# An experts' block in two stages: logits of all pairs first, most shared experts beside softmax and top-k

## The reference, cut to what matters

```
x = x + layernorm(mamba(layernorm(x)))          # ends with  y @ out_proj_w
h = layernorm(x)                                # (32, 256, 128)
scores = softmax(h @ gate_w.T)                  # 16 experts
topk_w, topk_idx = top_k(scores over the tokens, 32)
out = scatter_add of (gelu(x_tok @ Wg.T) * (x_tok @ Wu.T)) @ Wd.T * topk_w
shared = (gelu(h @ Ws_g.T) * (h @ Ws_u.T)) @ Ws_d.T
x = x + layernorm(out + shared)
layernorm(v) = (v - mean(v)) / sqrt(var(v) + 1e-5)
```

## Time and profile before

| | us |
|---|---|
| three runs | 1463.27 median (1461.69 to 1469.29) |
| the profiled execution | 1461.25 |
| its span, first to last instruction | 1459.2 |
| mamba and what is before it | 0 to 947.7 |
| the block under change | 947.7 to 1129.1 |
| gather, experts, scatter | 1129.1 to 1459.2 |

### The profile page before, as it was taken

How to read it: one execution, slowest core, us unless ns; L and a number is a source line. 1 busy time by engine, 2 the same in 40 slices (tenths; PEclk the granted TensorE clock), 3 DMA queues, 4 the chain that set the end, 5 groups by cost and what they waited for, 6 DMA issues and landing times. The chain is left out here.

```text
span 1459.2 us, 16108 instructions
## 1 busy us (share of the span) xinstructions
PE 1097.3 (75%) x4121; PEld 509.5 (35%) x4128; DVE 1149.3 (79%) x1531; ACT 887.4 (61%) x1588; POOL 862.9 (59%) x447
## 2 busy tenths in 40 slices
PE   4667777777778867877877865548886889999891
PEld 2312222222222222222222221125554336666791
DVE  6589999999999999999999999776757962222486
ACT  3656666666666666656656654324431876666894
POOL 0389989989989989989989989511101740000003
PEclk9979889889888889889889887769978999999896
DMA  5753853753752753753852755100000001111003
GB/s 153 170 113 69 173 108 69 172 108 68 172 111 65 172 110 66 172 108 68 172 111 66 173 110 122 57 12 1 1 0 1 21 1 35 41 33 42 0 0 115
DMA packets 48434, 122.76 MB, mean 84 GB/s; under 512 B 5776, under 2 KB 20880, under 8 KB 42256
## 3 DMA queue, kind: packets, MB, share of 16 engines
q1 hardware_dynamic: 46816, 121.01, 36.7%
q10 hardware_dynamic: 1584, 1.36, 0.3%
HBM read 83.55 MB, written 5.24 MB: 61 GB/s over the span
## 5 line engine op out<-in xcount | busy, mean ns | idle before, releaser
L551 POOL TENSOR_TENSOR states<-b_dup,dup 128x1024 f32<-128x1024 f32 x256 | 595.6, 2357 | 59.6 <-DMA dup<-dd 59.6
L638 DVE TENSOR_TENSOR_SCAN da<-da,states 128x1024 f32<-128x1024 f32 x176 | 396.2, 2284 | 51.0 <-ACT da L393 44.4
L393 ACT ACTIVATE da<-dup,decay 128x510 f32<-128x510 f32 x512 | 326.0, 671 | 0.0
L291 PE MATMUL yp<-states,fold 128*64 128x512 f32 x1024 | 274.5, 662 | 15.1 <-DVE states L570 8.8
L530 POOL TENSOR_TENSOR states<-states,X 128x1024 f32<-128x1024 f32 x80 | 188.1, 2351 | 92.0 <-DVE states L638 89.7
L570 DVE TENSOR_TENSOR states<-da,X 128x1024 f32<-128x1024 f32 x176 | 211.3, 1201 | 0.0
L389 ACT ACTIVATE da<-zeros 128x4 f32<-128x4 f32 x193 | 33.4, 173 | 289.9 <-DVE states L570 289.5
L638 DVE TENSOR_TENSOR_SCAN states<-da,states 128x1024 f32<-128x1024 f32 x80 | 182.5, 2282 | 14.0 <-ACT da L393 14.0
L1570 POOL TENSOR_TENSOR X<-X,xhT x4 | 12.0, 2995 | 250.3 <-DVE xhT L1550 250.3
L1428 DVE TENSOR_TENSOR hx<-glx,upx 128x512 f32<-128x512 f32 x64 | 41.3, 684 | 126.6 <-ACT glx L1393 118.2
L291 PEld LDWEIGHTS yp<-states,fold 128*64 128x64 f32 x1024 | 68.1, 148 | 206.4 <-issue 184.2
(11 more groups left out here) (184 smaller groups left out, 1798.5 us busy)
## 6 DMA issues: line engine op xcount, KB each, us to landing
b_dup<-bc_rows SPq DMA_DIRECT2D x32, 1024.0 KB, 9.6
dup<-dd SPq DMA_DIRECT2D x128, 256.0 KB, 10.4
X<-bc_rows SPq DMA_DIRECT2D x64, 512.0 KB, 8.8
out<-X SPq DMA_DIRECT2D x4, 1024.0 KB, 5.2
wg<-in_wgT SPq DMA_DIRECT2D x16, 128.0 KB, 2.1
wu<-in_wuT SPq DMA_DIRECT2D x16, 128.0 KB, 2.1
wd<-in_wdT SPq DMA_DIRECT2D x16, 128.0 KB, 2.2
bc_rows<-bcf SPq DMA_DIRECT2D x16, 64.0 KB, 1.6
```

The costliest lines, as they stand in the source:

```text
L291: last = nc.tensor.matmul(yp[64 * i:64 * i + 64, :], fold[:], states[:, (2 * step + i) % RING, s, :], start=False, stop=(q == 3 and s == S ...
L393: ins = nc.scalar.activation(factors[:, s, :].rearrange("p (b t) -> p b t", b=2)[:, :, 1:S], src[:, :, 1:S], ACT.Exp, scale=decay[:, col:c ...
L551: nc.gpsimd.tensor_tensor(states[:, i % RING], b_dup[:, par, s0:s0 + SPI, :], dup[:, par, 1, h, g, :].unsqueeze(1).broadcast_to([P, SPI, N ...
L638: nc.vector.tensor_tensor_scan(to.rearrange("p s t -> p (s t)"), factors.rearrange("p s t -> p (s t)"), ring.rearrange("p s t -> p (s t)") ...
```

## The change

Eight things are changed.

- In the Mamba block the mean over its 128 output columns is taken off each row of w_out, by four VectorE instructions at the program's start (semaphore `centred`). Each token's O then has mean zero, and the layer norm of O is a scaling.
- `statistics_o` makes only a variance; `norm_o` on VectorE is gone. Group 0 is done by 16 `scalar_tensor_tensor` on VectorE (X = O * rstd + X). Groups 1 to 3 are done on POOL, four `tensor_scalar` and one add per pair (`residual`).
- `statistics_o` runs ahead of its group: group 1 before the first pair, groups 2 and 3 after pairs 0 and 2.
- tp has two banks. The transposed pairs stay for all 16 pairs, in xhT at the place of O (`hT(n)`).
- Transposes and logits of all 16 pairs go first. Beside them TensorE does one shared pair in three (pairs 0 to 4; EARLY = 5).
- The other 11 shared pairs run beside softmax, top-k and the expansion of the indices. `down(m-1)` stands between the two halves of `gate_up(m)`.
- The slot matmuls stand before the last shared pair, and their PSUM place is in the bank of the logits.
- Loops are written out.

The diff, cut:

```diff
@@ mamba, VectorE
             nc.vector.tensor_scalar(decay[:], decay[:], 60.0, None, ALU.min).then_inc(decay_ready, 1)
+            nc.vector.tensor_reduce(w_mean[:], w_out[:], AX.X, ALU.add).then_inc(centred, 1)
+            dve.wait_ge(centred, 1)
+            nc.vector.tensor_scalar(w_mean[:], w_mean[:], 1.0 / DM, None, ALU.mult).then_inc(centred, 1)
+            dve.wait_ge(centred, 2)
+            for c in range(2):
+                nc.vector.tensor_scalar(w_out[:, c, :], w_out[:, c, :], w_mean[:, c:c + 1], None, ALU.subtract).then_inc(centred, 1)
@@ experts, POOL
+                def residual(g):
+                    pool.wait_ge(ro_ready, g + 1)
+                    pool.wait_ge(x_back[2 * g // G4], 16)
+                    for n in range(GP * g, GP * g + GP):
+                        for t in range(CH * n, CH * n + CH):
+                            o = O[:, t // 2, t % 2, :]
+                            nc.gpsimd.tensor_scalar(o, o, rstdo[:, t:t + 1], None, ALU.mult).then_inc(on_ready, 1)
+                        pool.wait_ge(on_ready, CH * (n - GP) + CH)
+                        gx = X[:, CH * n:CH * n + CH, :].rearrange("p (b c) d -> p b c d", c=2)
+                        nc.gpsimd.tensor_tensor(gx, gx, O[:, 2 * n:2 * n + 2], ALU.add).then_inc(x_ready, 1)
...
+                for g in range(1, G4):
+                    residual(g)
@@ experts, ScalarE
+                for n in range(PAIRS):
+                    g = n // GP
+                    turned(n)
+                    if n % GP == 1 and g < G4 - 1:
+                        nc.scalar.preload_act_table_set(LOG_EXP)
+                        inverse_x(g + 1)
+                        if g < G4 - 2:
+                            inverse_o(g + 2)
+                    if n % 3 == 2:
+                        for h in range(FH):
+                            gelu(n // 3, h)
+                    if n > 3 and n % 3 == 1:
+                        evacuate(n // 3 - 1)
@@ experts, VectorE
-                def norm_o(g):
-                    dve.wait_ge(ro_ready, g + 1)
-                    for t in range(GT * g, GT * g + GT):
-                        o = O[:, t // 2, t % 2, :]
-                        nc.vector.tensor_scalar(o, o, mvo[:, t, 0:1], rstdo[:, t:t + 1], ALU.subtract, ALU.mult
-                                                ).then_inc(on_ready, 1)
...
+                for t in range(GT):
+                    nc.vector.scalar_tensor_tensor(X[:, t, :], O[:, t // 2, t % 2, :], rstdo[:, t:t + 1], X[:, t, :],
+                                                   ALU.mult, ALU.add).then_inc(x0_ready, 1)
                 statistics_x(0)
+                statistics_o(1)
+                for n in range(PAIRS):
+                    g = n // GP
+                    norm(n)
+                    if n:
+                        take_logits(n - 1)
+                    if n > 3 and n % 3 == 1:
+                        products(n // 3 - 1)
+                    if n % GP == 1 and g < G4 - 1:
+                        statistics_x(g + 1)
+                    if n in (0, 2):
+                        statistics_o(2 + n // 2)
...
+                for r in range(rounds):
+                    products(EARLY + 1 + r)
+                    for g in range(GROUPS):
+                        round_of(r, g)
@@ experts, TensorE
+                turn(0)
+                for n in range(PAIRS):
+                    if n + 1 < PAIRS:
+                        turn(n + 1)
+                    logits(n)
+                    if n % 3 == 2:
+                        for h in range(FH):
+                            gate_up(n // 3, h)
+                    if n and n % 3 == 0:
+                        down(n // 3 - 1)
+                for m in range(EARLY, PAIRS):
+                    gate_up(m, 0)
+                    if m > EARLY:
+                        down(m - 1)
+                    gate_up(m, 1)
+                    if m == EARLY + 1:
+                        turn_scores()
+                    if m == PAIRS - 2:
+                        slots()
+                down(PAIRS - 1)
```

More of the change, by code:

```diff
@@ L805, in experts, with hT @@
             block = c.enter_context(nc.Block())
[L807 to L813, removed]
+            EARLY = (PAIRS - 1) // 3
+            def hT(n):
+                return xhT[:, 2 * n:2 * n + 2, 0:S]
             @block.sync
@@ L917, in _, with deviations @@
             def _(dve):
-                def statistics(g, which, source, s_ready, mvt, m_ready):
+                combined = iter(range(1, 100))
+                def deviations(g, source, s_ready):
+                    gs = slice(g * GT, (g + 1) * GT)
                     for t in range(GT * g, GT * g + GT):
@@ L952, in norm @@
+                    nc.vector.scalar_tensor_tensor(d_ap, d_ap, P / 4, d_ap, ALU.mult, ALU.mult).then_inc(comb_ready, 1)
+                    dve.wait_ge(comb_ready, next(combined))
+                    nc.vector.tensor_tensor(mvf[:, gs, 1], mvf[:, gs, 1], d_ap, ALU.add).then_inc(mx_ready, 1)
+                def norm(n):
+                    dve.wait_ge(rx_ready, n // GP + 1)
+                    if n > 1:
                         dve.wait_ge(tp_ready, n - 1)
                     for i in range(CH):
-                        ins = normed(dve, xf[:, par, i, :], CH * n + i)
+                        ins = normed(dve, xf[:, n % 2, i, :], CH * n + i)
@@ L1048, in _ @@
                                             best_f[:, g].unsqueeze(1).broadcast_to([P, E, CAP]), ALU.mult).then_inc(expanded, 1)
+                for m in range(EARLY + 2 + rounds, PAIRS):
+                    products(m)
                 dve.wait_ge(sl_ready, 1)
@@ L1088, in down @@
+                def down(m):
+                    pe.wait_ge(hs_ready, FH * m + FH)
+                    if m:
+                        pe.wait_ge(yp_free, m)
                     for i in range(CH):
@@ L1092, in down @@
                     mm.then_inc(yp_ready, 1)
-                def body(g):
-                    for k in range(GP):
-                        n, par = GP * g + k, k % 2
-                        logits(n, k)
-                        gate_up(n, k)
-                        if k < 3:
-                            turn(n + 1, 1 - par)
-                        down(n)
-                        if k == 3:
-                            turn(n + 1, 1 - par)
-                pe.wait_ge(wf_loaded, 64)
-                turn(0, 0)
```

281 lines of the change are left out of this document (113 added, 168 removed).

## The result

The changed kernel takes 1476.1 us (1470.2 to 1477.8, 16 runs), the kernel before 1465.5 beside it (1460.1 to 1469.3, 16 runs): ratio 1.0065, 95% interval 1.005 to 1.008. It is slower by 0.65%. The time lay in the forecast's range; its likeliest case, "within 0.5%", was missed on the slow side.

A forecast was written before the change was run, and what follows sets the result against it. Chains between engines, no full engine, bound the kernel. Walk -2.8, contention +3.5, clock +4.5, gather -1 sum to +4.2 on 1461.25: 1465.4; with 2.0 to the runs' median, 1467 us. Range 1452 to 1485.

The forecast's parts named there:

- within 0.5%: Whole kernel: time indistinguishable from no change, within about 0.5% or 7.3 us; the likeliest case, chance 0.41.
- The main claim: Block: 29.8 us gained up to the maximum's subtraction come back almost whole, as 7 more shared pairs at 5.4 are 37.8.
- The forecast's own sign of "slower": First part, up to the subtraction of the maximum: ending after 1070 would show the forecast wrong on the slow side.
- The walk: Step-by-step timing of the block: first part ends at 1058.6, evacuation at 1126.3, so the block ends 2.8 us earlier.
- The pace of top-k: Second part: three top-k rounds with products at 6.25 us each, then TensorE's 5.4 us per shared pair.
- the preamble: Block's start on VectorE: statistics and 16 fused adds (3.3 us) before the first norm, at 963.6 against 965.6 before.
- a forecast -1: Gather behind the block: may begin at the high clock instead of the low, -1 us, bounds -2 and 0.
- The POOL scaling: Groups 1 to 3 on POOL: a 128-wide scaling takes 0.33 us, bounds 0.2 and 0.77, so 10.6 us a group.
- slower, by POOL: Rival: scalings cost 0.6 or more, groups 15 us or more, group 1's 4.4 exposed; 1472 to 1475, chance with contention 0.14.
- Contention: First part: VectorE instructions slowed beside busy POOL, correction of 3.5 us, bounds 0 and 4.4.
- The clock: First part's steady stretch: TensorE partly at the low clock, 1.5 us for each of three triples, 4.5, bounds 0 and 10.5.
- The slots: Second part: slot matmuls behind dense work at the high clock, 4.0 us for four groups, against 1.8 a group before.

The follow-up runs named there:

- e6: The changed kernel with eight early shared pairs, one behind every second pair's logits, instead of five: 1464.7 us, ratio 1.0011 to the kernel before.
- e1: The changed kernel with POOL's four scalings of a pair made one 512-wide multiply with a broadcast operand: 1468.7 us, ratio 1.0042 to the kernel before.
- e7: The changed kernel with both eight early shared pairs and POOL's four scalings as one 512-wide multiply: 1464.8 us, ratio 1.0016 to the kernel before.
- e2: The changed kernel with extra matmuls, results unread, where TensorE waits for VectorE in the first part: 1466.0 us, ratio 1.0005 to the kernel before.
- e4: The kernel before, its order kept, with w_out centred and all 64 normalisations and adds as fused VectorE operations: 1447.6 us, ratio 0.988.
- e5: The changed kernel with all four groups' residuals as fused multiply-adds on VectorE, none on POOL: 1479.9 us, ratio 1.0118 to the kernel before.
- e9: As e8, but pair 11's gate and up stand straight behind its own logits: 1438.5 us, ratio 0.9837 to the kernel before.
- e8: e4 with two transpose banks and pair 11's shared work held back, its gate and up between the last logits: 1445.7 us, ratio 0.9896 to the kernel before.
- e3: The changed kernel with the slot matmuls moved behind the last shared pair's gate and up: 1471.8 us, ratio 1.0041 to the kernel before.
- e11: The kernel before with w_out centred and O's normalisation without mean subtraction; order and POOL's adds kept: 1453.3 us, ratio 0.9935.

## Why the prediction came out as it did

The main claim held: what leaves the first part comes back in the second. The forecast's own sign of "slower", a first part that ends after 1070, was met too: 123.7 us from the start at 947.7 are 1071.4. The walk had the second part at 67.7 us to the last evacuation (27.0 longer than before); measured, from 1069.8 to that evacuation's end near 1139.5, 69.7. Seven more shared pairs make it: at 5.22 us each they are 36.5, less the 8.2 us that TensorE had waited in front of the slots, as the forecast had it with 5.4 each. e6 shows the same from the other side by taking three pairs away. The pace of top-k (6.2 and 5.22, forecast 6.25 and 5.4) was right as well, and the preamble nearly: the first norm comes 16.7 us into the block, in the walk 15.9, as the 16 fused adds took 4.29 us for 3.3. The gather's -0.9 for a forecast -1 proves nothing, as it lies within what the profiles vary by.

The first part came out at 123.7 where the walk had 110.9 and its corrections added 8. By milestones from the block's start:

- **The POOL scaling, mis-sized.** I took 0.33 us, near a quarter of the add, from bounds of 0.2 and 0.77. It is 0.6 (median 602 ns). Group 1 took 14.6 us for 10.6, so the statistics of x started at 32.1 for 27.2: 4.1 us beyond the 0.8 that the preamble was late. This is the largest term that was mis-sized, and the rival "slower, by POOL" described it at its place and size (4.4 exposed). The rule of the Trainium skill, "GPSIMD Engine Reference", Engine selection, that one-input work on GpSimd is roughly line-rate, would have made it shorter still; the 617 ns of 128 elements beside 1178 ns of a 512-wide two-input add speak against it for instructions this small.
- **Contention, a little too high.** Forecast 3.5; the profile has one small addition at 1.17 and one pair of norms 0.7 longer, and up to the second gate/up only 1.9 us were lost in all, part of it to the clock. What the Trainium skill describes in "SBUF — State Buffer", Who interferes with whom, that one of the two engines waits while the other holds the ports they share, fits e1 and e7 better: beside POOL's 512-wide multiply and add four norms took 3.7 and 4.2 us, for 1.11 alone. No run shows that the ports are the reason.
- **The clock, right in kind.** I had 4.5 for three triples, bounds 0 and 10.5. The three gate/ups there took 5.3, 4.9 and 6.1 for 3.45, and this stretch was 6.0 us over the walk, all of it in them. With fillers (e2) they took 3.5 each. That e2's first part is also 6.0 us shorter is chance: 2.3 of these lie before this stretch.
- **The slots.** They took 5.0 for 4.0, and the clock that fell among them made gate/up and down behind them longer. The walk had assumed that busy work before them keeps the level.

With 4.1 for POOL, 0.8 for the preamble and 2.0 for the second part the forecast of +4.2 becomes +11.1, which is what block and gather measured together (12.0 less 0.9). That it closes so well is partly luck: contention was put 1.6 us too high (3.5 for 1.9) and the clock 1.5 too low (4.5 for 6.0), and the two cancel. The sign of the likeliest case was right, its distance from zero less than half of the measured.

What the prediction did not ask is what the first part would be without the stages. It credited the shorter first part to the change as a whole. e4 shows that the cheaper normalisation alone brings it, because before the change the long block of normalisations on VectorE starved TensorE three times, and behind two of these waits the clock fell; e5 shows that with the same arithmetic as e4 the stages lose 2.4%. The expected gain went into TensorE's idle time: five pairs are too few to fill it in front of the softmax, and eleven fill the second part to the brim.

## What to carry to other kernels

When work is postponed to shorten a chain, count the idle time of the engine that does this work in both stages: here a shared pair cost 2.1 us where it filled TensorE's gaps and at least 5.2 where TensorE was full. Try the cheap arithmetic in the old order before a new order; it may remove by itself the wait that the new order is meant to avoid. And put independent matmuls into the wait (e9), not between the pieces that others wait for (e8): it was the same work, and a difference of 7 us.

## What the runs showed of the hardware

- A scaling of 128 elements per partition with a scalar from a tile takes 0.6 us on POOL (48 in the changed kernel, median 602 ns), a 512-wide multiply 1.04 (e1) and a 512-wide add 1.18: three quarters of the length save half of the time or less.
- A fused multiply-add on VectorE with three tile operands took 0.27 us for 128 elements in a row of 16, with POOL idle; the statistics beside it 0.20.
- The granted clock fell to the low level among 8-column matmuls, in the third or fourth set of slots, while TensorE was busy without a gap (changed kernel, e3). In the profiles of e1 and e6 it did not fall there, and in e7 only behind the fourth set (up 1.81 and down 2.86 us for 1.02 and 1.95); why is open.
- In TensorE's steady work idle times of 2.70 (kernel before) and 2.91 us (e8) were followed by the low clock. Of two of 2.78 us in the kernel before, one was and one was not. Idle times of 1.60, 1.53, 1.38 and 0.87 us were not (e11, e8), but one of 1.51 us behind lighter work was (e5: the down at 1066.77 took 3.58 us). The length of the wait alone does not tell.
